# Silu on ScalarE for two tiles at a time, an eighth of the products by C on VectorE, expert tiles one unit sooner, and the transfers before the loop in another order

## The reference

```python
xn = layernorm(x)
# branch 1: tokens sorted by cluster, then a selective scan over each sequence of 2048
scores  = einsum('bnd,kd->bnk', l2norm(xn), l2norm(means))     # 8 clusters
xs      = xn sorted by argmax(scores)
x_dbl   = einsum('bdl,cd->bcl', xs^T, x_proj_weight)           # dts 32, Bm 16, Cm 16
delta   = softplus(einsum('brl,dr->bdl', dts, dt_projs_weight) + dt_projs_bias)
h_t     = exp(delta_t * A) * h_{t-1} + (delta_t * u_t) * B_t   # 256 channels x 16 states
y_t     = sum over the 16 states of h_t * C_t, + D * u_t       # C = Cm + prompt of the cluster
# branch 2: a mixture of 8 experts, the best 2 of each token
h = silu(xn @ w1[e]) * (xn @ w3[e]);  y = h @ w2[e]            # 256 -> 512 -> 256
out = x + unsorted(branch 1) + probability-weighted sum of the two experts
```

## Time and profile before

| what | value |
|---|---|
| median of three runs | 806.15 us (804.61 to 807.02) |
| the profiled execution's own time | 806.1 us |
| its span in the profile | 804.4 us |
| mean granted TensorE clock | 0.934 of full |
| VectorE busy | 681.4 us, 85% |
| TensorE busy | 656.8 us, 82% |
| GpSimd busy | 597.1 us, 74% |
| ScalarE busy | 420.1 us, 52% |
| bytes moved | 116.97 MB, mean 145 GB/s |

### The profile page before, as it was taken

One profiled execution on the slowest core, in us unless ns is written; L12 is line 12 of the kernel. 1 busy time (PEld: TensorE's weight loads), 2 busy tenths in 40 slices (PEclk: granted clock), 3 DMA queues, 4 the chain that ended last, 5 costly groups with the idle time before them and its releaser, 6 DMA issues.

```text
span 804.4 us, 13844 instructions
## 1 busy us (share of the span) xinstructions
PE 656.8 (82%) x4602; PEld 429.7 (53%) x4602; DVE 681.4 (85%) x883; ACT 420.1 (52%) x910; POOL 597.1 (74%) x371
## 2 busy tenths in 40 slices
PE   2733976578888799987989898898989888989993
PEld 1513754335555565655556555555556555655662
DVE  5868856699999999999999999999989998997120
ACT  1323665575566555655556555655546564653231
POOL 3727820057788899898989989998988889899542
PEclk9975988789999899999999999999989998999997
DMA  7972659999846743754484466547546643532332
GB/s 213 371 279 92 188 185 302 306 274 247 215 95 137 163 92 96 164 134 93 109 180 107 93 142 143 119 109 159 111 81 152 154 94 82 115 67 40 47 40 26
DMA packets 66275, 116.97 MB, mean 145 GB/s; under 512 B 12104, under 2 KB 46496, under 8 KB 64160
## 3 DMA queue, kind: packets, MB, share of 16 engines
q1 hardware_dynamic: 44048, 88.78, 39.2%
q0 software_dynamic: 19824, 27.16, 19.5%
q10 hardware_dynamic: 2336, 0.15, 0.2%
HBM read 80.78 MB, written 35.27 MB: 144 GB/s over the span
## 4 chain that ended last, share of the span: by engine, by line
DVE 35%; POOL 26%; issue 14%; DMA 11%; PE 10%; ACT 2%; SPq 0%; another core or an unknown queue 0%; DVEq 0%; POOLq 0%; ACTq 0%
DVE ring L965 19%; POOL ring L461 12%; DVE pb L956 10%; DMA out_dram<-pool,tab 6%; POOL out_dram L448 4%; POOL out_dram L455 4%; POOL pool L441 3%; DVE pool L997 2%; POOL xs_d L417 2%; DMA ring<-in_L_attn_x_dram 2%; PE py L1215 2%; DMA ring<-xs_d 2%; POOL w2x L424 1%; ACT ring L608 1%; PE fa L1204 1%
## 5 line engine op out<-in xcount | busy, mean ns | idle before, releaser
L461 POOL TENSOR_TENSOR ring<-ring,bc 128x1024 f32<-128x1024 f32 (+1 forms) x127 | 306.0, 2428 | 27.5 <-DVE state L972 25.5
L965 DVE TENSOR_TENSOR_SCAN ring<-ring,state,pb 128x512 f32<-128x512 f32 x256 | 313.8, 1267 | 5.0 <-ACT ring L608 0.4
L608 ACT ACTIVATE ring<-late,aneg 128x512 f32<-128x512 f32 x256 | 164.4, 726 | 0.0
L956 DVE TENSOR_TENSOR pb<-fb,bc 128x1024 f32<-128x1024 f32 x128 | 157.3, 1229 | 2.2
L1215 PE MATMUL py<-w2x,pool 128*128 x568 | 144.4, 400 | 0.0
L448 POOL DMA_INDIRECT out_dram<-pool,tab x71 | 113.6, 1601 | 37.3 <-DMA out_dram<-pool,tab 25.0
L1204 PE MATMUL fa<-w,pool 128*128 x284 | 136.1, 602 | 2.0 <-ACT pool L668 2.0
L1204 PE MATMUL fb<-w,pool 128*128 x284 | 134.6, 596 | 0.7 <-DVE pool L1000 0.7
L441 POOL DMA_INDIRECT pool<-xn_d,tab x71 | 71.5, 1007 | 76.8 <-PE fb L1092 34.1
L1215 PEld LDWEIGHTS py<-w2x,pool 128*128 128x128 f32 x568 | 110.2, 205 | 13.8
L1137 PE MATMUL py<-ring,fold 128*32 128x128 f32 x2048 | 70.9, 280 | 26.8 <-POOL ring L461 26.8
(11 more groups left out here) (211 smaller groups left out, 717.6 us busy)
## 6 DMA issues: line engine op xcount, KB each, us to landing
late<-dd_d SPq DMA_DIRECT2D x256, 128.0 KB
bc<-bc_d SPq DMA_DIRECT2D x64, 256.0 KB
w<-in_L_ffn_w_dram SPq DMA_DIRECT2D x16, 512.0 KB, 8.0
ring<-in_L_attn_x_dram SPq DMA_DIRECT2D x8, 512.0 KB, 4.4
out_dram<-ring SPq DMA_DIRECT2D x8, 512.0 KB, 7.1
xn_d<-w2x SPq DMA_DIRECT2D x8, 512.0 KB, 8.3
dd_d<-pool SPq DMA_DIRECT2D x8, 512.0 KB, 5.0
dd_d<-ring SPq DMA_DIRECT2D x8, 512.0 KB, 6.1
```

Source lines behind the costliest of these rows:

```text
L461: return po.tensor_tensor(r, r, bc[:, u // G % 2, 1, states, :].rearrange("p n c -> p (n c)"), ALU.mult)
L608: ins = ac.activation(ring[:, u % RING, n, :], dd[:, u % 2, 0, :], ACT.Exp, scale=aneg[:, NH * g + n:NH * g + n + 1])
L956: ve.tensor_tensor(pb[:, :].rearrange("p (n c) -> p n c", n=2), pd[:, :].rearrange("p (o c) -> p o c", o=1).to_broadcast([P, 2, CH]), bc[: ...
L965: ve.tensor_tensor_scan(r, r, pb[:, CH * m:CH * m + CH], state[:, NH * g + n:NH * g + n + 1], ALU.mult, ALU.add).then_inc(S["scan_done"], 1)
```

## The change

ScalarE computes silu itself in place of tanh, so that VectorE has one multiplication left of `silu`, from the gate in SBUF and `fb` in PSUM. Silu and exp lie in two tables of functions, so the table is changed by `preload_act_table_set` between them. From tile 3 on the gates of tiles j and j+1, j odd, are computed in one iteration, with one load of each table for the pair, and TensorE computes the first product of tile j+1 before the second product of tile j. The last 256 of a unit's 2048 columns are multiplied by C on VectorE (`share`, in the next unit) and no longer on GpSimd. VectorE does `silu(u)` in unit u, so every list of tiles stands one unit sooner against the units, and seven tiles are left for the tail. Three experts are loaded before the loop; `load_bc` of chunk 0 comes in the first pass of the list; the other five experts' w3 and w2 are issued together after `load_dd(2)`.

```diff
-REST = UNITS + 1
+REST = UNITS + 2
+SINGLE = 3
+SHARE = 256
-EARLY = 2
+EARLY = 3
...
         @block.sync
             for c in range(NCH):
+                if c == 1:
+                    sp.wait_ge(S["inv_step"], NGRP)
+                    load_up(0, w3, w3_in)
                 if c + 3 < NCH:
                     load_sorted(c + 3)
...
+                    load_down(0)
+                if c in (3, 4):
...
                     load_up(c - 2, w3, w3_in)
                     load_down(c - 2)
+                if c + 1 < NCH:
+                    store_bc(c + 1)
+                if c == 0:
+                    sp.wait_ge(S["bc_put0"], 32)
+                    sp.wait_ge(S["etab_ready"], 1)
+                    for q in range(P // DG):
+                        load_bc(0, q)
+                if c == NCH - 2:
                     for h in range(KC):
                         sp.wait_ge(S[f"dd_put0{h}"], 16)
                     load_dd(0)
+                store_dd(c)
+                if c == NCH - 2:
                     load_dd(1)
...
             for u in range(UNITS):
                 if u >= 2:
                     load_dd(u)
-                if c == 0 and EARLY <= g:
-                    load_up(g, w3, w3_in)
-                    load_down(g)
+                if u == 2:
+                    for e in range(EARLY, E):
+                        load_up(e, w3, w3_in)
+                        load_down(e)
...
         @block.gpsimd
-                j = u - 2
+                j = u - 1
...
                 if u < UNITS - 1:
-                    done = multiply(u, slice(split, NH))
+                    done = multiply(u, slice(split * CH, NH * CH - SHARE))
...
         @block.scalar
-            def tanh(j):
+            def gate(j):
                 ac.wait_ge(S["a_done"], j + 1)
-                ac.activation(sg[:, j % 2, :], fa[j % 2][:, :], ACT.Tanh, scale=0.5).then_inc(S["tanh_done"], 1)
+                if j >= 2:
+                    ac.wait_ge(S["htr_done"], j - 1)
+                ac.activation(sg[:, j % 2, :], fa[j % 2][:, :], ACT.Silu).then_inc(S["gate_done"], 1)
...
+            for j in range(1, FT):
+                u = j
+                first = j < SINGLE or j % 2
+                if first:
+                    ac.preload_act_table_set("silu_and_others")
+                    gate(j)
                 if u < UNITS:
                     put_du(u)
+                evac_ht(j - 1)
+                if first:
+                    if j >= SINGLE:
+                        gate(j + 1)
+                    if u + 1 < UNITS:
+                        ac.preload_act_table_set("exp_and_others")
...
         @block.vector
             def silu(j):
-                ve.wait_ge(S["tanh_done"], j + 1)
+                ve.wait_ge(S["gate_done"], j + 1)
+                ve.wait_ge(S["b_done"], j + 1)
                 t = sg[:, j % 2, :]
-                ve.scalar_tensor_tensor(t, t, 1.0, fa[j % 2][:, :], ALU.add, ALU.mult).then_inc(S["s1_done"], 1)
-                ve.wait_ge(S["s1_done"], j + 1)
-                ve.wait_ge(S["b_done"], j + 1)
-                ve.scalar_tensor_tensor(t, t, 0.5, fb[0][:, :], ALU.mult, ALU.mult).then_inc(S["silu_done"], 1)
+                ve.tensor_tensor(t, t, fb[0][:, :], ALU.mult).then_inc(S["silu_done"], 1)
+            def share(u):
+                ve.wait_ge(S["h_ready"], u + 1)
+                r = ring[:, u % RING, NH - 1, CH - SHARE:CH]
+                ve.tensor_tensor(r, r, bc[:, u // G % 2, 1, NH - 1, CH - SHARE:CH], ALU.mult).then_inc(S["hd_done"], 1)
             for u in range(UNITS):
                 if u:
-                    silu(u - 1)
+                    silu(u)
+                    share(u - 1)
                 half_unit(u, 0)
+                if u == 0:
+                    silu(u)
                 half_unit(u, 1)
...
         @block.tensor
             def fold_states(u):
+                else:
+                    pe.wait_ge(S["hd_done"], u + 1)
...
             for j in range(1, FT):
-                u = j + 1
+                u = j
-                up(j, e_up)
-                if j < REST:
+                if j < SINGLE:
+                    up_gate(j, e_up)
+                    up_value(j, e_up)
+                    turn_h(j - 1)
+                elif j % 2:
+                    up_gate(j, e_up)
+                    turn_h(j - 1)
+                    up_gate(j + 1, e_next)
+                    up_value(j, e_up)
+                else:
+                    up_value(j, e_up)
                     turn_h(j - 1)
```

More of the change, by code:

```diff
@@ L238, in apart, with x_turned @@
             eng.sem_inc(S["passed"], 1)
+        def x_turned(j):
+            return py if j == 0 else pt if j <= REST else pb
         def experts_by(u):
-            return max(0, u - 1)
-        LAST_SCANS = UNITS - 1
+            return max(0, u)
+        LAST_SCANS = UNITS
         def scans_by(u):
@@ L481, in _ @@
                 po.wait_ge(S["h_ready"], u + 1)
-                done = multiply(u, slice(0, split))
+                done = multiply(u, slice(0, split * CH))
                 for n in scans:
@@ L491, in _ @@
                     add_expert(j)
-            for j in range(UNITS - 2, FT):
+            for j in range(UNITS - 1, FT):
                 if j + XR < FT:
@@ L636, in take_sum, with evac_xt @@
                 ac.copy(y1[:, :], pz[:, 256:384]).then_inc(S["y1_done"], 1)
+            def evac_xt(j):
+                ac.wait_ge(S["xtr_done"], j + 1)
+                if j == 2:
+                    ac.wait_ge(S["dd_put00"], 16 * NCH // 2)
+                ac.copy(xt[j % XT], x_turned(j)[:, 0:D]).then_inc(S["xt_done"], 1)
             def weigh(g):
@@ L689, in _ @@
             ac.sem_inc(S["ye_done"], 1)
-            evac_xt(0)
             put_du(0)
             exps(0)
-            tanh(0)
+            gate(0)
+            evac_xt(1)
+            ac.preload_act_table_set("exp_and_others")
             exps(1)
-            for u in range(1, FT + 1):
-                j = u - 1
-                if j:
-                    tanh(j)
+            for j in range(1, FT):
[4 more added lines that the diff above has]
+                    gate(j)
                 if u < UNITS:
                     put_du(u)
-                if j:
-                    evac_ht(j - 1)
+                evac_ht(j - 1)
[3 more added lines that the diff above has]
+                    if u + 1 < UNITS:
+                        ac.preload_act_table_set("exp_and_others")
                 if 3 <= u < UNITS + 3:
@@ L706, in _ @@
                     take_sum(u - 2)
-                if j + 1 < FT:
-                    evac_xt(j + 1)
+                ahead = j + 1 if j < SINGLE else j + 2
+                if ahead < FT:
+                    evac_xt(ahead)
                 if u + 1 < UNITS:
                     exps(u + 1)
-                if j:
-                    evac_y(j - 1)
+                evac_y(j - 1)
+                if j == SINGLE - 1:
+                    evac_xt(j + 2)
             evac_ht(FT - 1)
@@ L1016, in _ @@
                              ALU.mult).then_inc(S["hc_last"], 1)
-            for j in range(UNITS - 1, FT):
+            for j in range(UNITS, FT):
                 silu(j)
@@ L1173, in turn_x @@
                 for k in range(KC):
[L1174 removed]
+                    ins = pe.transpose(x_turned(j)[:, P * k:P * k + P], xr[j % XR][:, P * k:P * k + P],
                                        ident[:, :])
@@ L1188, in turn_h @@
                 pe.wait_ge(S["silu_done"], j + 1)
+                ahead = j + 2 if j + 1 < SINGLE else j + 3
+                pe.wait_ge(S["xt_done"], min(ahead, FT))
                 for k in range(HC):
@@ L1226, in _ @@
             e_down = expert_of(0)
-            up(0, e_down)
+            pe.wait_ge(S["pr_ut"], KC * (NCH - 1))
+            up_gate(0, e_down)
+            up_value(0, e_down)
+            pe.wait_ge(S["pr_ab"], KC * NCH)
+            pe.wait_ge(S["pr_re"], KC * NCH)
+            pe.wait_ge(S["pr_xd"], NCH)
             turn_x(1)
@@ L1230, in _ @@
             for j in range(1, FT):
-                u = j + 1
+                u = j
+                e_next = expert_of(j + 1) if j + 1 < FT else None
                 if j == G + 1:
```

83 lines of the change are left out of this document (36 added, 47 removed).

## The result

The changed kernel takes 875.62 us (873.38 to 877.82, four runs) where the kernel before took 805.38 beside it (799.79 to 807.02, four runs): 1.089 times as long, 95% interval 1.085 to 1.093. The forecast was 792 and the range ended at 808. The profiled execution's span is 871.3 us against 804.4.

| stage | before | changed | forecast |
|---|---|---|---|
| to unit 0's last reduce | 169.67 | 160.53 | -8.5 + 0.6 |
| 63 units | 567.4 | 648.4 | -23 + 16 + 4.5 |
| from unit 63's last reduce to the end | 67.3 | 62.4 | -4.4 |
| span | 804.4 | 871.3 | 790.4 |

What follows compares the result with a forecast made beforehand. VectorE was taken to set the loop's pace. Terms -23.0 + 0.6 + 16 - 8.5 + 4.5 - 4.4 = -14.8, taken as -14, gave 792 us; range 781 to 803, with two rivals 774 to 808.

Steps and rivals of the forecast that it cites:

- VectorE's period: VectorE in the loop: two silu instructions out, two multiplications in, 8.53 us per unit, -23.0 us over 63 units.
- GpSimd: nothing by itself: GpSimd's product by C shrinks by an eighth, 0.59 us for 256 columns; no gain counted by itself.
- TensorE's waits: In the loop, silu waits for TensorE after late folds (g = 6), 3.8 to 3.9 us per chunk: +16 us net.
- ScalarE: hidden: ScalarE's table loads, 1.30 us each, and silu at 0.60 us fit into its waits; no time added.
- The third rival: ScalarE becomes the bound: a table change holds it twice the 1.28 us, kernel slower at 818 us; chance 0.13.
- The start and the first units: Before the loop: first scan near 154 to 155, -8.5 us; in the first units, waits for transfers, +4.5 us.
- the bound of -12: Limit of the gain at the start (-8.5 taken, -3 the other bound), if only the 18.0 us chain counts.
- the 18.0 us chain alone: Start: the stretch from the last rows' landing to the first scan, 18.0 us, without transfers in the way.
- The tail: After the last reduce: one scatter and one TensorE iteration fewer, -4.4 us, bounds 0 and -6.
- TensorE didn't catch up: Rival for the loop: folds of g = 6 early enough or clock stays up, VectorE waits no more, 776 us; chance 0.25.
- the second rival: Transfers eat the start: first scan only 3 us sooner, unit 3 waits 8 us, 801 us; chance 0.15.

Runs made afterwards that it cites:

- The run in pieces: Changed kernel with GpSimd's product by C cut into instructions of 256 columns in place of 1024 and 768: 824.21 us, ratio 1.029.
- the run with three places: Changed kernel, late weights one expert per unit, VectorE's product by C between halves, before the first half's scans or at unit start, by unit: 793.46 us, ratio 0.983.

## Why the prediction was wrong

**VectorE's period: the step that failed.** It said "And one of 128x256: 426 ns, less the 0.08 that such instructions overlap, 0.345". The row is right for what it shows, an instruction in the work before the loop with GpSimd at rest, and it was carried to a place where GpSimd works. The other parts of the sum hold: without the instruction the period is 8.19, and 8.19 + 0.345 = 8.53 is found in the changed kernel itself wherever the product met nothing. Measured, the 63 cost 122.1 us less 5 of overlap, 117 in place of 21.7: +95. "GpSimd: nothing by itself" failed with it. The new instruction had a bound from below and none from above; how GpSimd's product beside it bears on it was never asked. What the runs showed in its place is a wait: 1.94 us in the mean, up to 4.5, until GpSimd's product is out. The section "SBUF: two separate sides" of the Trainium skill, named above, has the rule that would have made a rival of it. Both streams start at one semaphore, so the wait could have been priced: one 1024-column instruction more per unit, 63 x 2.365 = 149 us, is an estimate on the high side of the 95 that came.

**The sum of the loop.** 63 x 8.53 = 537.4, and 95 for the waits, 7.6 for unit 3 beyond its neighbours and 3.7 for TensorE's second product beside its longest wait make 643.7 of the 648.4; the other 4.7 I didn't take apart.

**TensorE's waits: right in the mean, and hidden by the failure.** With VectorE at 10 us per unit TensorE is on time. Where the collision was taken away the forecast came true: in the run with the operand in PSUM units 8c+9 are late by 4.7, 5.5, 1.1, 2.3, 4.1 and 3.2 us, 21.0 against 23 forecast, and no other unit behind the first three by over 0.5. The sum fits better than its parts: 3.8 to 3.9 were forecast for each chunk. TensorE's timeline of that run, chunk 4, from the fold of unit 38 (whose reduce began at 515.68), VectorE's silu of unit 41, and the window (us, busy of five engines, granted clock, DMA share, GB/s):

```profile
524.11 1.42 PE L1174 MATMUL py<-ring,fold 128*32 128x128 f32 x32 [2.35 <-POOL ring L476]
...
529.52 1.88 PE L1234 MATMUL fa<-w,pool 128*128 x4
531.24 0.60 PE L1229 MATMUL pt<-ident,pool 128*128 128x128 f32 x4
531.67 1.88 PE L1234 MATMUL fa<-w,pool 128*128 x4
533.39 1.88 PE L1234 MATMUL fb<-w,pool 128*128 x4
```

```profile
535.38 0.69 DVE L1025 TENSOR_TENSOR pool<-pool,fb 128x512 f32<-128x512 f32 x1 [2.26 <-PE fb L1234]
```

```profile
524.00:528.00 4.00, 3.56 (x40) 2.71 (x41) 3.90 (x7) 2.10 (x6) 3.35 (x4) 0.59 0.63 135
```

The fold comes 8.43 us after the reduce (8.7 forecast), TensorE had idled 2.35, the granted clock is 0.59 just behind that, so part of the stretch is at the 1.2 GHz level, and from fold to first product it takes 5.41 us in place of 4.02 (5.97 forecast).

**ScalarE: hidden, as forecast.** Timeline of the changed kernel, ScalarE, a pair; it answers to the earlier trace rows:

```profile
180.98 2.56 ACT L621 ACTIVATE ring<-late,aneg 128x512 f32<-128x512 f32 x4 [8.51 <-DMA late<-dd_d]
...
406.32 1.28 ACT L718 ACT_TABLE_LOAD   x1
407.62 0.60 ACT L691 ACTIVATE pool<-fa 128x512 f32<-128x512 f32 x1
...
409.69 0.60 ACT L691 ACTIVATE pool<-fa 128x512 f32<-128x512 f32 x1 [0.30 <-PE fa L1233]
410.30 1.28 ACT L727 ACT_TABLE_LOAD   x1
```

A load takes 1.28 us and the gate starts 1.30 after it; silu takes 0.60. The third rival, a change of table that holds ScalarE for twice the 1.28 us, doesn't hold here: 68 loads at L718 and L727, none with more than 0.02 us of idle time before it. The 2.66 us that the Trainium skill, "ScalarE: Activation LUTs", section "What ACT_TABLE_LOAD costs", gives for a change don't show.

**The start and the first units.** First scan at 153.84 (154 to 155 forecast): the time is right, the path isn't. The forecast had it hang on `load_dd(0)` landing near 150.5. In the changed kernel's chain of waits it hangs on the last rows, which land at 137.63 (139 forecast), and on the work behind them:

```profile
130.25 7.38 DMA ring<-xs_d
...
150.29 0.60 ACT fb L632
150.89 2.48 ACT ring L621 x4
```

ScalarE's copy of delta*u at 150.29 waits for no transfer. The stretch from the rows to the first scan took 16.2 us where it had taken 18.0; no term said so, and 139 with the 18.0 would have given 157.0. So the agreement is in part luck, and the bound of -12 for "the 18.0 us chain alone" doesn't follow from its numbers either (157.0 is -6.4).

The first row of ScalarE's timeline above is unit 3's exponentials, late by a wait of 8.51 us for delta, as forecast in place and cause; the gate of tile 3 stands behind them in ScalarE's queue, and VectorE's silu in unit 3 waits the 9.3 us of the waits above; the size was high in the range of 0 to 10 where 4 was put, 7.6 us in the changed kernel, and just outside it, 10.6 to 11.4, in the runs in which the weights were not spread and the product waited little or not at all, where VectorE is there sooner.

**The tail.** 62.4 us, within the 62 to 63 forecast.

Of the rivals, TensorE didn't catch up (21 us of waits once the collision was gone), and the transfers did cost what the second rival gave unit 3 (8 us), but the first scan came at the time forecast.

So all terms but one were within 9 us. The run with the PSUM operand has that one at its price and still gives 805 and not 792. Its span is 14.7 us above the forecast: 8.5 in units 1 and 3, 7 in a period of 8.64 in place of 8.53 (it has one wait more), about 1 in single units, less 2 in TensorE's waits.

## What to carry to other kernels

Before work is moved from one engine to another, look for what the two share: the duration of an instruction on a quiet chip is its lower bound. Here VectorE's product with both inputs in SBUF waited out GpSimd's product, which reads SBUF, and it showed as a long instruction, not as idle time; so compare the mean duration of a shape with its shortest. If it can't be avoided, put one operand in PSUM, or place it where the other engine's timeline is free, unit by unit; here this took the kernel from 8.9% above the kernel before to 3.5% below it, together with the weights and the scatters.

## What the runs showed of the hardware

VectorE's product waits behind both of GpSimd's product instructions in 13 cases and behind the first alone in 22. Which it is goes by how GpSimd came to them: all 13 follow right on its gather, as at 411.50; all 22 follow a wait for VectorE's reduce, as at 423.59. There the second instruction waits in turn, 0.17 us. The run in pieces has the extreme of it: once seven pieces follow right on the gather, from 626.83, and VectorE's product, begun at 627.16, takes 4.78 us and ends behind all seven. The run with 512 columns has an exception: at 622.51 the pair follows 0.03 us behind the gather, and VectorE is let in behind the first. Why instructions that stand ready mostly hold VectorE off like one long instruction, these runs don't tell. The section of the Trainium skill named above has the other engine wait for one instruction; in these 13 cases the wait is longer.

Nor is it always the one that is listed first that has its way. In the kernel before with the product added, 12 of VectorE's products begin 0.26 to 0.69 us ahead of GpSimd's, while GpSimd's gather is still running, and would be over in 0.42; they take 4.67 to 5.09 us and end behind both. The first of them, and GpSimd beside it:

```profile
291.23 4.95 DVE L1006 TENSOR_TENSOR ring<-ring,bc 128x256 f32<-128x256 f32 x1
```

```profile
290.73 1.01 POOL L443 DMA_INDIRECT pool<-xn_d,tab  x1 [0.30 <-issue]
291.76 4.13 POOL L463 TENSOR_TENSOR ring<-ring,bc 128x1024 f32<-128x1024 f32 x2
```

By the Trainium skill's rule the one that starts first would have had the ports; by these start times, which are rough on GpSimd, it didn't. So a place just ahead of GpSimd's product isn't free either. A gather or a scatter with no product right behind it doesn't hold VectorE off: in the run with three places two products begin inside such a gather and 31 inside a scatter, and all take 0.40 to 0.42 us.

What makes the move of the scatters worth 12 us of the 63 units in one pair of kernels (where the product's places moved with it), 4 in the pair with the PSUM operand and 2.6 in the pair without the product stays open.
